# Pass one's layer in three split products with its weight's halves in the experts' tiles, and the correlation with its operands swapped

## The reference

```python
# 1: autocorrelation, with Q = layernorm(x), K = V = context, channel by channel
corr = ifft(fft(q) * conj(fft(k))).real          # 64 lags for each channel
w, idx = top_k(corr, 8); w = softmax(w)
out = sum_i w_i * v[min(pos + idx_i, 63)]
# 2: a linear layer with eight low-rank adapters
x @ W.T + bias + sum_n (x @ A_n.T) @ (B_n * coef_n).T
# 3: grouped-query cross attention (32 heads, 8 for keys and values) with the context
# 4: relu(x @ up)**2 @ down + (x @ fc1 @ expert @ fc2) * (sum of the top 2 logits), and a layernorm
```

## Time and profile before

| | |
|---|---|
| median of 3 runs | 746.63 us (743.79 to 748.07) |
| the profiled execution's own time | 746.08 us |
| its span, first to last instruction | 744.2 us |
| mean granted TensorE clock | 0.975 |
| PE busy | 688.0 us (92%) |
| DVE, ACT, POOL busy | 496.2, 494.3, 369.7 us |

### The profile page before, as it was taken

How to read it: one execution, slowest core, us unless ns; L and a number is a source line. 1 busy time by engine, 2 the same in 40 slices (tenths; PEclk the granted TensorE clock), 3 DMA queues, 4 the chain that set the end, 5 groups by cost and what they waited for, 6 DMA issues and landing times.

```text
span 744.2 us, 12239 instructions
## 1 busy us (share of the span) xinstructions
PE 688.0 (92%) x3834; PEld 473.2 (64%) x3834; DVE 496.2 (67%) x1125; ACT 494.3 (66%) x881; POOL 369.7 (50%) x445
## 2 busy tenths in 40 slices
PE   8789999999987749799999999999999999999874
PEld 3344554545443437577877878878878878876663
DVE  3787878787742875676776776777677767756411
ACT  3567767675724978678688687697787786784110
POOL 1347777765534232443663563564554555554422
PEclk9999999999999979999999999999999999999997
DMA  7234444352212120101101101101101101000000
GB/s 242 87 99 129 114 141 123 110 174 77 85 57 103 43 79 22 43 1 58 42 16 57 42 14 56 42 14 56 42 14 56 42 14 56 14 15 29 0 15 29
DMA packets 25781, 45.69 MB, mean 61 GB/s; under 512 B 3184, under 2 KB 4976, under 8 KB 25744
## 3 DMA queue, kind: packets, MB, share of 16 engines
q1 hardware_dynamic: 25744, 45.24, 19.0%
HBM read 36.84 MB, written 8.39 MB: 61 GB/s over the span
## 4 chain that ended last, share of the span: by engine, by line
PE 85%; DVE 5%; ACT 5%; issue 3%; POOL 1%; POOLq 0%; DVEq 0%; ACTq 0%
PE ps_b L991 9%; PE ps_b L992 8%; PE ps_b L993 8%; PE wide L1088 7%; PE wide L991 4%; PE ps_b L1029 4%; PE wide L993 4%; PE wide L992 4%; PE bank L1059 4%; PE ps_a L1029 4%; PE wide L1049 4%; PE ps_b L1172 4%; PE ps_a L991 2%; PE ps_a L993 2%; PE ps_a L992 2%
## 5 line engine op out<-in xcount | busy, mean ns | idle before, releaser
L608 POOL TENSOR_TENSOR va<-mv,small 128x1 f32<-128x1 f32 x80 | 15.3, 191 | 141.4 <-DVE mv L971 81.8
L420 ACT ACTIVATE q_stack<-qt_h 32x512 fp32r<-32x512 f32 x128 | 80.6, 630 | 1.9
L688 POOL TENSOR_TENSOR y_l<-y,y_h 128x512 fp32r<-128x512 f32 x16 | 20.6, 1290 | 97.5 <-ACT y_h L550 97.5
L1088 PE MATMUL wide<-w_m,x1t 128*128 128x512 f32 x128 | 60.8, 619 | 0.7 <-ACT x1t L441 0.7
L991 PE MATMUL ps_b<-down_h,ht_h 128*128 128x512 f32 x128 | 53.9, 421 | 6.2 <-DVE ht_l L893 3.4
L900 DVE RECIPROCAL y<-ps_b 128x256 f32<-128x256 f32 x32 | 55.9, 1748 | 0.0
L991 PE MATMUL wide<-up_h,t_h 128*128 128x512 f32 x128 | 52.3, 408 | 1.2 <-DVE t_l L880 1.2
L677 POOL TENSOR_TENSOR kbd_b<-kt_h,small 128x512 bf16<-128x512 f32 x32 | 34.1, 1086 | 35.7 <-ACT kt_h L519 35.7
L993 PE MATMUL ps_b<-down_h,ht_l 128*128 128x512 f32 x128 | 51.2, 400 | 0.0
L992 PE MATMUL ps_b<-down_l,ht_h 128*128 128x512 f32 x128 | 50.9, 398 | 0.0
L993 PE MATMUL wide<-up_h,t_l 128*128 128x512 f32 x128 | 50.6, 396 | 0.0
(11 more groups left out here) (193 smaller groups left out, 2075.9 us busy)
## 6 DMA issues: line engine op xcount, KB each, us to landing
x_in<-in_x SPq DMA_DIRECT2D x16, 256.0 KB, 2.7
ctx_t<-in_ctx SPq DMA_DIRECT2D x16, 256.0 KB, 2.6
x_res<-in_x SPq DMA_DIRECT2D x16, 256.0 KB, 2.6
x_in<-x_rows SPq DMA_DIRECT2D x16, 256.0 KB, 2.7
ctx_t<-in_ctx_turned SPq DMA_DIRECT2D x16, 256.0 KB, 2.9
x_res<-x_rows SPq DMA_DIRECT2D x16, 256.0 KB, 3.6
out<-stage SPq DMA_DIRECT2D x16, 256.0 KB, 2.0
x_rows<-x SPq DMA_DIRECT2D x8, 256.0 KB, 2.4
```

Of the source, the lines that this page charges most:

```text
L420: last = act.activation(out[STACK * part:STACK * (part + 1), p, :], halves[STACK * p:STACK * (p + 1), :].bitcast(F32), ACT.Copy)
L1088: last = pe.matmul(bank[7], cols(x1t, c, P), cols(w0_m, c, D), start=(c == 0), stop=(c == DC - 1))
```

## The change

The layer of pass one becomes a split product. Its weight's sum is kept in place in w0_sum, and its halves w0_h and w0_l lie in the tiles rt_h and rt_l: ScalarE makes the high halves and GpSimd the low ones, in turn -2. x1t is split too: ScalarE copies bank 5 twice (into fp32r and into f32), GpSimd subtracts. The correlation has icorr as the stationary operand and 512 columns of prod moving, twice, with an output of 64 partitions each; its result has lags on partitions, so ScalarE copies it to a new tile lags, and four transposes turn it back into bank 4, from which VectorE reads it as before. These transposes stand behind V on TensorE.

```diff
--- before.py
+++ after.py
@@ -167,13 +167,14 @@
         ex_t, fc2_raw = one("ex_t", [P, 2, LAT]), one("fc2_raw", [P, 2, D])
         ex_fc2, fc1_t = one("ex_fc2", [P, 2, D]), one("fc1_t", [P, 2, D])
         dft = one("dft", [P, DFT])
-        w0_m = one("w0_m", [P, DC * D])
+        w0_h, w0_l = rt_h, rt_l
         b0_all = one("b0_all", [P, D])
         first = one("first", [P, FIRST])
         icorr = first[:, ICORR0:ICORR0 + SEQ]
         iout = [first[:, IOUT0 + SEQ * j:IOUT0 + SEQ * (j + 1)] for j in range(2)]
         coef, coef_scaled = one("coef", [P, 1]), one("coef_scaled", [P, 1])
         qf, prod = one("qf", [P, 2 * D]), one("prod", [P, 2, D])
+        lags = one("lags", [P, D])
         m8 = one("m8", [P, 2 * DC, TOP])
         kept_not = one("kept_not", [P, 2 * DC, SEQ])
         weight = one("weight", [P, 2 * DC, SEQ + TOP])
@@ -188,6 +189,7 @@
         xn2 = one("xn2", [P, D])
         blank = xn2
         x1t = one("x1t", [P, D])
+        x1t_h, x1t_l = one("x1t_h", [P, D], F32R), one("x1t_l", [P, D], F32R)
         bn1, mv1, va1, rs1 = one("bn1", [P, 6]), one("mv1", [P, 2]), one("va1", [P, 1]), one("rs1", [P, 1])
         nm1, nb1, nm2, nb2 = (one(n, [P, 1]) for n in ("nm1", "nb1", "nm2", "nb2"))
         bn2, mv2, va2, rs2 = one("bn2", [P, 6]), one("mv2", [P, 2]), one("va2", [P, 1]), one("rs2", [P, 1])
@@ -231,12 +233,12 @@
             t4_ps t4_hi t4_lo u_ps relu_s h_s top_s rw_s rt_out_ps routed_s
             ht_ps ht_hi ht_lo dn_ps z_s zg_s o_s
             blank_s const_in dft_loaded first_in merge_in lora_in w0_in gate_in bcast_in stage_in stage_odd_in gate_split
-            coef_ready bt_ready ef_ps ef_ready w0_ps w0_add rt_ps rt_hi rt_lo
+            coef_ready bt_ready ef_ps ef_ready w0_ps w0_add w0_hi w0_lo rt_ps rt_hi rt_lo
             stage_hi stage_lo
             nm1_s nb1_s nm2_s nb2_s x_loaded ctx_loaded res_loaded bn1_s mv1_s va1_s rs1_s xn1_s
-            q_ps qf_s k_ps prod_s v_ps vf_s vsw_s corr_ps tops_s shift_s exp_s rep_s sum_s inv_s sub_s wgt_s
+            q_ps qf_s k_ps prod_s v_ps vf_s vsw_s corr_ps lag_s lag_ps tops_s shift_s exp_s rep_s sum_s inv_s sub_s wgt_s
             wt_ps wt_s wf_ps prod2_s o_ps x1_s bn2_s mv2_s va2_s rs2_s xn2_s
-            xt_ps xt_s ffn_ps x2_raw x2_res x2_s x2_stored x2_odd_stored""".split()
+            xt_ps xt_s xt_lo ffn_ps x2_raw x2_res x2_s x2_stored x2_odd_stored""".split()
         S = {name: sem(name) for name in SEMS}
         x2_stored = (S["x2_stored"], S["x2_odd_stored"])
 
@@ -438,6 +440,8 @@
                 if live(t):
                     act.wait_ge(S["xt_ps"], t + 1)
                     wait(act, S["ffn_ps"], t)
+                    act.activation(x1t_h[:], bank[5], ACT.Copy)
+                    wait(act, S["xt_lo"], t)
                     act.activation(x1t[:], bank[5], ACT.Copy).then_inc(S["xt_s"], 1)
                 t = i + 2
                 if live(t):
@@ -454,11 +458,15 @@
                     hi, part = PIECES[n][1], PIECES[n][3]
                     act.wait_ge(stage_in[n % 2], LANDED[n])
                     if n == FIRST_UP:
-                        act.wait_ge(S["w0_add"], DC)
+                        act.wait_ge(S["w0_lo"], DC)
                         act.wait_ge(S["gate_split"], 2)
                     act.activation(cols(hi, part, PIECE), stage[n % 2][:], ACT.Copy).then_inc(S["stage_hi"], 1)
                 if early(i):
                     context_high(0)
+                t = i + 2
+                if live(t):
+                    act.wait_ge(S["corr_ps"], t + 1)
+                    act.activation(lags[:], bank[4], ACT.Copy).then_inc(S["lag_s"], 1)
                 t = i + 1
                 if live(t):
                     act.wait_ge(S["wt_ps"], t + 1)
@@ -496,6 +504,10 @@
                     query_high(0)
 
             def peeled(i):
+                if i == -2:
+                    for c in range(DC):
+                        act.wait_ge(S["w0_add"], c + 1)
+                        act.activation(w0_h[:, c, 0:D], w0_sum[:, c, :], ACT.Copy).then_inc(S["w0_hi"], 1)
                 if i == -1:
                     act.wait_ge(S["gate_in"], 16)
                     act.activation(rt_h[:, :, D:], gate_raw[:], ACT.Copy).then_inc(S["gate_split"], 1)
@@ -630,6 +642,11 @@
                     pool.wait_ge(S["inv_s"], t + 1)
                     pool.tensor_tensor(wgt[:], wgt[:], total_inv[:].unsqueeze(2).to_broadcast([P, 2 * DC, SEQ]), ALU.mult
                                        ).then_inc(S["wgt_s"], 1)
+                t = i - 1
+                if live(t):
+                    pool.wait_ge(S["xt_s"], t + 1)
+                    wait(pool, S["ffn_ps"], t)
+                    pool.tensor_tensor(x1t_l[:], x1t[:], x1t_h[:].bitcast(F32), ALU.subtract).then_inc(S["xt_lo"], 1)
                 n = piece_of(i)
                 if n is not None:
                     hi, lo, part = PIECES[n][1:]
@@ -647,6 +664,11 @@
                     wait(pool, S["xn1_s"], t)
                     normaliser(t, mv1, va1, rs1, nm1, nb1, 1)
                 if i == -2:
+                    for c in range(DC):
+                        pool.wait_ge(S["w0_hi"], c + 1)
+                        pool.tensor_tensor(w0_l[:, c, 0:D], w0_sum[:, c, :], w0_h[:, c, 0:D].bitcast(F32), ALU.subtract
+                                           ).then_inc(S["w0_lo"], 1)
+                if i == -1:
                     pool.wait_ge(S["bcast_in"], 16 * 7)
                 t = i - 2
                 if live(t):
@@ -815,7 +837,7 @@
                 t = i + 2
                 if live(t):
                     corr = bank[4].rearrange("p (c s) -> p c s", s=SEQ)
-                    dve.wait_ge(S["corr_ps"], t + 1)
+                    dve.wait_ge(S["lag_ps"], t + 1)
                     for c in range(2 * DC):
                         top = dve.max(m8[:, c, :], corr[:, c, :])
                     top.then_inc(S["tops_s"], 1)
@@ -841,7 +863,7 @@
                     dve.wait_ge(S["w0_in"], 16)
                     for c in range(DC):
                         dve.wait_ge(S["w0_ps"], c + 1)
-                        dve.tensor_tensor(cols(w0_m, c, D), bank[LORA_BANK[c]], w0_sum[:, c, :], ALU.add
+                        dve.tensor_tensor(w0_sum[:, c, :], bank[LORA_BANK[c]], w0_sum[:, c, :], ALU.add
                                           ).then_inc(S["w0_add"], 1)
                 if i == -1:
                     dve.wait_ge(S["gate_split"], 1)
@@ -1053,10 +1075,8 @@
                 if live(t):
                     pe.wait_ge(S["prod_s"], t + 1)
                     wait(pe, S["shift_s"], t)
-                    for c in range(DC):
-                        for b in range(2):
-                            k = slice(P * c + SEQ * b, P * c + SEQ * (b + 1))
-                            last = pe.matmul(bank[4][:, k], prod[:, b, P * c:P * (c + 1)], icorr, start=True, stop=True)
+                    for b in range(2):
+                        last = pe.matmul(bank[4][SEQ * b:SEQ * (b + 1), :], icorr, prod[:, b, :], start=True, stop=True)
                     last.then_inc(S["corr_ps"], 1)
                 t = i + 1
                 if live(t):
@@ -1071,6 +1091,10 @@
                 t = i + 2
                 if live(t):
                     transform(ps_b, V0, ctx_t).then_inc(S["v_ps"], 1)
+                    pe.wait_ge(S["lag_s"], t + 1)
+                    for c in range(DC):
+                        last = pe.transpose(cols(bank[4], c, P), cols(lags, c, P), ident)
+                    last.then_inc(S["lag_ps"], 1)
                 if early(i, 1):
                     queries(0)
                 t = i + 1
@@ -1080,12 +1104,13 @@
                     transform(ps_a, W0, wt).then_inc(S["wf_ps"], 1)
                 t = i - 1
                 if live(t):
-                    pe.wait_ge(S["xt_s"], t + 1)
+                    pe.wait_ge(S["xt_lo"], t + 1)
                     wait(pe, S["x2_raw"], t)
                     if t == 0:
-                        pe.wait_ge(S["w0_add"], DC)
-                    for c in range(DC):
-                        last = pe.matmul(bank[7], cols(x1t, c, P), cols(w0_m, c, D), start=(c == 0), stop=(c == DC - 1))
+                        pe.wait_ge(S["w0_lo"], DC)
+                    for c in range(DC):
+                        last = split_product(bank[7], cols(x1t_h, c, P), cols(x1t_l, c, P), w0_h[:, c, 0:D], w0_l[:, c, 0:D],
+                                             c == 0, c == DC - 1)
                     last.then_inc(S["ffn_ps"], 1)
                 if early(i):
                     keys_values(0)
```

## The result

The changed kernel takes 770.22 us (median of 4 runs, 768.68 to 773.8) against 745.21 (4 runs): a ratio of 1.032, interval 1.028 to 1.036. It is slower, by 25 us by the medians and 24 by the profiled spans. I had forecast 763, alone 759 to 768, with a range of 751 to 771: the time lies outside the narrow figures and 0.8 us inside the wide one.

A forecast was written before the change was run, and what follows sets the result against it. TensorE was full at 12.145 us a turn; after the change a ring of engine orders would bind at 13.09. Eleven turns 10.4, start 4.4, turns 0 and 1 1.0, end 1.2: 17.0 on 746.08, so 763, range 751 to 771.

The forecast's parts named there:

- a clock that falls in the steady turns: Rival: TensorE's clock falls as its gaps grow to 1.9 us a turn, adding 10 us: 773; chance 0.10.
- TensorE gets lighter and the turn longer: Pass one's turns: TensorE's work 1.0 us less (layer 0.64, correlation 0.91, transposes -0.54), yet turns 13.09 against 12.145.
- The ring: Pass one, product to next product: 5.82 us to exp plus 7.27 through ScalarE to the product, 13.09 a turn.
- The collision: GpSimd's add blocks VectorE's short subtraction L826: 0.75 us in place of 0.24; turn 13.09 against 12.45 without it.
- the turns with a piece: Nine turns with a piece of a weight: normalisers up to half a us later; same 0.94 us more taken.
- the later L471: In turns with a piece, L471 on late normalisers may hold up exp; otherwise it allows exp at P + 4.85.
- The start: Weight halves in turn -2 delay tile 0's softmax weights and exp: 4.4 us, plus 1.0 for turns 0 and 1.
- The end: End of pass one: 0.9 (turn 14) - 0.64 (tile 13's layer) + 1.8 - 0.9 (last layer), 1.2 us more.
- The last two terms: Last layer: waits 1.8 us for two ScalarE copies and GpSimd's subtraction; its twelve shorter instructions take 0.9 less.
- The ring without the collision: Rival: small shifts part the add and L826, turns of 12.45 us, 757 us; chance 0.25.
- TensorE as the bound: Rival: ScalarE's copies and the turned lags find slack, 11.15 us a turn, kernel faster at 741 us; chance 0.05.

The follow-up runs named there:

- lags_early: Changed kernel with the new transposes of the lags ahead of V on TensorE; 756.94 us, 1.013 of the kernel before.
- piece_late: Changed kernel with the low half of a weight's piece made behind the two adds on GpSimd; 772.87 us, 1.030 of the kernel before.
- adds_wait: Changed kernel with GpSimd's two adds held until the short subtraction is done; 760.33 us, 1.021 of the kernel before.
- corr_only: Kernel before with only the correlation swapped, its lags copied and turned, the layer still f32; 753.31 us, 1.010 of the kernel before.
- all_moves: Changed kernel, transposes ahead of V, adds behind subtraction, weight halves in turn 0, x's low half on VectorE, piece behind adds; 738.52 us, 0.988 of before.

## Why the prediction was right, point by point

- **The time.** 770.2 lies at the edge of the range, and in part by luck. The profiled span missed +17.0 by 6.8: 3.8 in the turns, 3.6 at the end, 1.2 at the start, less the 1.8 by which pass two happened to be shorter, which nobody forecast. The range reached to 771 for a clock that falls in the steady turns, and it did not fall there.
- **TensorE gets lighter and the turn longer.** Right, but lighter by the layer alone. I took 0.91 - 0.54 = 0.37 us off for the swapped correlation; from its start to the layer's start it is 4.30 us before and after. I had priced the new blocks and not what they do to their neighbours. The layer gave 0.65, as forecast (0.64), so TensorE's work fell by at most 0.65 and not by 1.0 (by 0.25 in the busy column), and it was idle for 1.0 to 1.7 us a turn, not for 1.9.
- **The ring.** Right in its course: product, correlation, L1088 and V, new transposes, maxima, exp, ScalarE's chain. TensorE's part was mis-sized: 3.41 us from the product to the maxima in place of 3.13, because the correlation took 1.01, L1088 0.59 and V 1.06, where the earlier trace rows had 0.93 (half of L1049), 0.54 and 0.96. The chain from exp to the product was 7.23 against 7.27. In the turns without a piece the total, 12.92 against 13.09, is closer than its terms: the subtraction came 0.31 later than forecast (5.20 us after the product, not 4.89), and the add ended 0.11 earlier (5.58, not 5.69), so that the collision cost 0.25 us in place of 0.64.
- **The collision.** Right: L848 took 1.17 us in the turns with a piece and 0.46 without, and with the adds held back 0.22. The Trainium skill, in "SBUF — State Buffer", section "SBUF: two separate sides", says that the loser "fully blocks"; the runs agree, since the subtraction ended 0.08 us after the GpSimd operation in each of the collisions shown (rows of the turn above, of lags_early and of piece_late).
- **The term that was mis-sized: the turns with a piece.** I took 13.09 for all turns. Measured were 12.92 without a piece and 13.63 with one. I had said that there the add would start about where L826 does, and "either the collision or the later L471" holds up exp. It started 0.2 us ahead, which is nearly the worst place: most of the add was still to come. Eight turns at 0.54 more and three at 0.17 less make 3.8 us, the whole difference between +14.2 and +10.4.
- **The start.** Right in place and nearly in size, 6.6 against 5.4; the maxima came at 32.28 against 31.1, although the softmax weights were ready 0.9 sooner than I had put them (28.0 against 28.9): L1088, V and the transposes ran at half clock, 1.04, 2.02 and 1.04 us from start to start, about twice what I had summed.
- **The end.** 4.8 against 1.2, the step that missed most for its size. I counted one layer at half clock, the last. Turn 14's softmax weights came 1.2 us later than before (forecast 0.9), and TensorE waited 2.5 us ahead of L1088. The blocks from there through most of tile 13's layer then ran at half clock: that layer, which I had 0.64 shorter, took 4.45 us (231.73 to 236.18, when ScalarE copies its result) against 3.73, and the blocks ahead of it lost the rest of 2.1 us. The last two terms were nearly right: the last layer's start came 2.0 later (1.8), and it was 0.6 shorter (0.9). So 1.2 + 2.1 + 2.0 - 0.6, where I had 0.9 - 0.64 + 1.8 - 0.9. The cold clock was a rival of mine in the steady turns, where it did not come (1.00); it came at both ends.
- **The rivals.** The ring without the collision would have given 12.68 us a turn (adds_wait, 760 us). TensorE as the bound is refuted by its 1.0 to 1.7 us of idle time in each turn of the changed kernel, and by adds_wait, which leaves TensorE's work as it is and shortens the turns; not by corr_only, where TensorE got no lighter.

## What to carry to other kernels

When one engine is full and the others are not, taking work off it is a gain only as far as the ring of orders around it allows: write down the chain from one turn's product to the next, with every block that merely stands in between, before adding a hand-off to it. Here a copy, a transpose block behind V and a second copy made a ring of 12.7 us (the collision not counted) around some 11.5 us of TensorE work, and five edits to the order, one of which drops a copy, turned 3.2% slower into 1.2% faster. Price a changed block together with its neighbours: here the correlation became 0.83 us shorter and the stretch around it did not. And look at where a GpSimd operation falls beside a short VectorE operation with two SBUF inputs: a few hundredths of a us decide whether the short one takes 0.2 us or 1.3.

## What the runs showed of the hardware

- The short subtraction took 0.21 to 0.25 us where no add or piece was under way on GpSimd, and 0.45, 0.75, 1.17, 1.33 and 2.32 us where one had 0.4 to 2.2 us left. Its neighbour (L847 in the changed kernel), which reads PSUM, took 0.69 in every full turn, also where the add ran beside it (4.59 to 5.28 us after the product, the add from 4.28 on).
- A block of four f32 instructions of 512 columns on half the rows takes 0.96 us from start to start beside another of its kind, and 1.06 where it stands between transposes (V: 151.13 to 152.19). In all_moves, with V next to the weights' transform again, it is 0.96 (142.35 to 143.31).
- TensorE's gaps of 0.9, 0.2 and 0.7 us a turn left the granted clock at 1.00; gaps of 2.5 to 3.2 us at the start and end were followed by stretches at 0.52 and 0.61. The length of the last gap does not settle it: before, the last layer ran at 0.50 behind gaps of 1.3 us (ahead of L1097 at 223.78) and 0.7.
